# LayerNorm's turned rows from a second layout of x: a broadcast by DMA, a subtraction on GpSimd, a product on VectorE

## What is computed

```python
mod = (silu(c) @ wmod).reshape(2, 6, 1, -1)      # sa, ca, ga, sb, cb, gb
h = layernorm(x) * (1 + ca) + sa
q, k, v = silu(h @ wq), sigmoid(h @ wk), h @ wv
f = 1 - k                                        # decay; its sign against 0.5 gives the rotation
S = S * f + k * v; o = q * scale @ S             # scanned over 4096 rows, 4 heads of 128
out = layernorm(o * sigmoid(h @ wg1 @ wg2)) * norm_w @ wo
x = x + ga * out
h = layernorm(x) * (1 + cb) + sb
xr, xk = mixes of h and h shifted by one row
x = x + gb * sigmoid(xr @ W_r) * (relu(xk @ W_k)**2 @ W_v)
```

## Time and profile before

| | |
|---|---|
| median of 3 runs | 1790.52 us |
| profiled execution, time | 1790.45 us |
| profiled execution, span (first to last instruction) | 1788.9 us |
| TensorE's granted clock, mean | 0.999 of full speed |
| attention part | about 44 to 1193 us of the span |
| channel mix | from there to the end |

### The profile page before, as it was taken

How to read it: one execution, slowest core, us unless ns; L and a number is a source line. 1 busy time by engine, 2 the same in 40 slices (tenths; PEclk the granted TensorE clock), 3 DMA queues, 4 the chain that set the end, 5 groups by cost and what they waited for, 6 DMA issues and landing times.

```text
span 1788.9 us, 45434 instructions
## 1 busy us (share of the span) xinstructions
PE 1761.1 (98%) x18909; PEld 1583.4 (89%) x18909; DVE 1523.5 (85%) x3483; ACT 829.6 (46%) x1493; POOL 364.4 (20%) x303
## 2 busy tenths in 40 slices
PE   9999999999999999999999999998999999999999
PEld 7888888988999888988999889987888888989888
DVE  7898988989899899989899898998878777787875
ACT  4444444444444445444444444444454545454453
POOL 1000111101110011101110011102334343434443
PEclk9999999999999999999999999999999999999999
DMA  6122113211221112311121111210221212111110
GB/s 236 49 61 60 37 37 80 53 37 37 43 62 41 37 37 55 102 37 37 43 55 48 37 37 43 67 49 36 83 71 49 71 48 71 52 67 60 60 60 36
DMA packets 107700, 102.02 MB, mean 57 GB/s; under 512 B 65748, under 2 KB 67560, under 8 KB 107496
## 3 DMA queue, kind: packets, MB, share of 16 engines
q1 hardware_dynamic: 107480, 99.11, 19.3%
q10 hardware_dynamic: 16, 0.00, 0.0%
HBM read 48.77 MB, written 34.60 MB: 47 GB/s over the span
## 4 chain that ended last, share of the span: by engine, by line
PE 85%; DVE 9%; ACT 3%; issue 3%; DVEq 0%; ACTq 0%
PE bank L1336 60%; PE lvl L1336 9%; ACT hF L467 3%; PE bank L1450 3%; PE bank L1344 2%; PE bank L1443 2%; PE lvl L1411 2%; PE bank L1442 1%; PE bank L1434 1%; DVE xs L813 1%; DVE hT_hi L760 1%; DVE og L951 1%; PE lvl L1394 1%; PE lvl L1429 1%; DVE A L936 1%
## 5 line engine op out<-in xcount | busy, mean ns | idle before, releaser
L133 POOL TENSOR_TENSOR ln_rs<-ln_ve,mhalf 128x2 f32<-128x2 f32 x64 | 82.8, 1294 | 875.0 <-DVE ln_ve L128 875.0
L1336 PE MATMUL bank<-hT_hi,wq_hi 128*128 128x256 f32 x512 | 147.3, 288 | 11.9 <-DVE og L951 10.7
L402 POOL COPY og_halves<-og 128x1024 uint16<-128x1024 uint16 x60 | 65.3, 1089 | 407.8 <-DVE og L951 407.8
L1336 PE MATMUL bank<-hT_hi,wk_hi 128*128 128x256 f32 x512 | 148.2, 289 | 0.0
L1336 PE MATMUL bank<-xk_hi,fk_hi 128*128 128x256 f32 x512 | 145.1, 283 | 0.6 <-DVE xk_lo L1008 0.6
L1336 PE MATMUL bank<-hT_lo,wk_hi 128*128 128x256 f32 x512 | 144.9, 283 | 0.0
L1336 PE MATMUL bank<-xk_hi,fk_lo 128*128 128x256 f32 x512 | 144.9, 283 | 0.0
L1336 PE MATMUL bank<-xk_lo,fk_hi 128*128 128x256 f32 x512 | 144.9, 283 | 0.0
L1336 PE MATMUL bank<-hT_lo,wq_hi 128*128 128x256 f32 x512 | 144.7, 283 | 0.0
L1336 PE MATMUL bank<-hT_hi,wq_lo 128*128 128x256 f32 x512 | 144.7, 283 | 0.0
L1336 PE MATMUL bank<-hT_hi,wk_lo 128*128 128x256 f32 x512 | 144.7, 283 | 0.0
(11 more groups left out here) (234 smaller groups left out, 5754.0 us busy)
## 6 DMA issues: line engine op xcount, KB each, us to landing
xs<-in_L_attn_x SPq DMA_DIRECT2D x32, 512.0 KB, 4.0
x_scratch<-xs SPq DMA_DIRECT2D x32, 512.0 KB, 2.9
xs<-x_scratch SPq DMA_DIRECT2D x32, 512.0 KB, 3.6
out<-xs SPq DMA_DIRECT2D x31, 512.0 KB, 2.8
mod_raw<-in_L_wmod SPq DMA_DIRECT2D x6, 1024.0 KB, 7.2
raw_q<-in_L_attn_wq SPq DMA_DIRECT2D x2, 512.0 KB, 4.8
raw_k<-in_L_attn_wk SPq DMA_DIRECT2D x1, 1024.0 KB, 6.3
raw_v<-in_L_attn_wv SPq DMA_DIRECT2D x1, 1024.0 KB, 7.5
```

The source lines that it names most:

```text
L133: pool.tensor_tensor(out=ln["rs"][:, :], in0=ln["ve"][:, :], in1=mhalf[:, :], op=ALU.pow).then_inc(ln["rstd"], 1)
L402: pool.tensor_copy(halves[:, ch, :].rearrange("p (two e) -> p two e", two=2), og[n % 2][:, ch, :].bitcast(U16).rearrange("p (e two) -> p t ...
L1336: last = pe.matmul(dst, lhs(a, s), rhs(b, s), start=(t == 0), stop=(t == len(terms) - 1))
```

## The change

- x is also given in a second layout, turned (512 x 8192), made on the host. SP loads block n + 2 of it straight into `hF` (`xT_load`), behind the load of x.
- The statistics move up: `ln_stats` and `ln_var` for block n + 2 now stand after the second `joined_low`, before `pair_update(n, 1)`.
- Mean and 1/std of the 256 rows lie beside each other in `mvr`. SP writes them to DRAM as 512 single numbers, waits for that, and reads them back broadcast to all 128 partitions (`spread_rows`), 2 KB each.
- GpSimd subtracts the mean from `hF` in one pass of 128x1024 (`h_normal`), VectorE multiplies by 1/std in one pass of 128x1024 (`h_product`) where `apply_next` stood, ScalarE applies scale and shift in place (`h_scaled`).
- `t1` and `ln_apply` are kept only for blocks 0 and 1 and for the channel mix, whose first turning is still made in body 30.
- On TensorE the query pair 1 (bank 3) is computed before pair 0 (bank 2), and the wait for `og_sb` stands between them; ScalarE and VectorE take the pairs in that order too (`place`).

```diff
+                def xT_load(n):
+                    sp.wait_ge(h_lo, n)
+                    sp.dma_start(hF[:, :, :], xT[:, rows(n)].rearrange("(k p) t -> p k t", p=P)).then_inc(xT_in, 16)
+
+                def spread_rows(n):
+                    sp.wait_ge(ln["rstd"], n + 1)
+                    sp.wait_ge(h_lo, n)
+                    sp.dma_start(rowd[n].rearrange("(v p) -> p v", p=P), ln["mvr"][:, :, 0], allow_slow_non_contiguous=True).then_inc(row_out, 16)
+                    sp.wait_ge(row_out, 16 * (n - 1))
+                    sp.dma_start(mr[:, :, :].rearrange("p q t -> p (q t)"),
+                                 rowd[n].unsqueeze(0).to_broadcast([P, 2 * TB])).then_inc(mr_in, 16)
...
                         ln_load(sp, ln, xf if n + 2 < NB else x2d, n + 2)
+                    if n + 2 < NB:
+                        xT_load(n + 2)
...
+                    if n + 2 < NB:
+                        spread_rows(n + 2)
                     if n < LAST - 1:
                         turn_og(n, 0)
...
+                def h_normal(n):
+                    pool.wait_ge(xT_in, 16 * (n - 1))
+                    pool.wait_ge(mr_in, 16 * (n - 1))
+                    pool.tensor_tensor(out=hF[:, :, :], in0=hF[:, :, :], in1=mr[:, 0, :].unsqueeze(1).to_broadcast([P, KT, TB]),
+                                       op=ALU.subtract).then_inc(h_off, 1)
...
                     ln_rstd(pool, ln, mhalf, n + 2)
+                    if n + 2 < NB:
+                        h_normal(n + 2)
                     if n < LAST - 1:
                         og_split(n, 0)
...
+                def h_scaled(n):
+                    act.wait_ge(h_norm, n - 1)
+                    for k in range(KT):
+                        act.activation(hF[:, k, :], hF[:, k, :], ACT.Identity, scale=scl[0][:, n // BPB, k:k + 1],
+                                       bias=sft[0][:, n // BPB, k:k + 1]).then_inc(h_full, 1)
...
+                def h_product(n):
+                    dve.wait_ge(h_off, n - 1)
+                    dve.tensor_tensor(out=hF[:, :, :], in0=hF[:, :, :], in1=mr[:, 1, :].unsqueeze(1).to_broadcast([P, KT, TB]),
+                                      op=ALU.mult).then_inc(h_norm, 1)
...
+                    q_silu(n + 1, 1 - par, 1)
+                    joint(n, 1)
                     q_silu(n + 1, 1 - par, 0)
-                    joint(n, 1)
-                    q_silu(n + 1, 1 - par, 1)
                     if n > 0:
                         joined_low(n - 1, 1)
+                    ln_stats(dve, ln, n + 2)
+                    wait(dve, row_out, 16 * n)
+                    ln_var(dve, ln, n + 2)
                     pair_update(n, par, 1)
...
-                    dve.wait_ge(mm["t1"], 2 * (n + 2))
+                    if n == 0:
+                        dve.wait_ge(mm["t1"], 4)
                     f_signed(n + 1, 1 - par, 0, xn[:, 0, :])
...
-                    ln_stats(dve, ln, n + 2)
-                    ln_var(dve, ln, n + 2)
                     first_totals(n + 1)
...
-                    apply_next(n + 2)
+                    if n + 2 == NB:
+                        apply_next(n + 2)
+                    elif n + 2 < NB:
+                        h_product(n + 2)
...
                     pe.wait_ge(h_lo, n + 2)
+                    wait(pe, s_mid, n)
+                    rows_of("q", 1, 2, "q")
+                    if n == 0:
+                        mod_rows(2, bank[0])
                     wait(pe, og_sb, 2 * n)
                     rows_of("q", 0, 2, "q")
-                    wait(pe, s_mid, n)
-                    if n == 0:
-                        mod_rows(2, bank[0])
-                    rows_of("q", 1, 2, "q")
...
-                    pe.wait_ge(kt_sb, kept(n, chunks_kept(n) - 1))
-                    pe.wait_ge(gate_sb, 2 * (n + 1) + 1)
-                    t1(n + 2)
+                    if n + 2 == NB:
+                        pe.wait_ge(kt_sb, kept(n, chunks_kept(n) - 1))
+                        pe.wait_ge(gate_sb, 2 * (n + 1) + 1)
+                        t1(n + 2)
```

More of the change, by code:

```diff
@@ L51, with adaln_kernel @@
 XS = 4
-def adaln_kernel(nc, x, wq, wk, wv, wo, wg1, wg2, norm_w, W_r, W_k, W_v, mu_r, mu_k, c, wmod, out):
+def adaln_kernel(nc, x, xT, wq, wk, wv, wo, wg1, wg2, norm_w, W_r, W_k, W_v, mu_r, mu_k, c, wmod, out):
     xf = x.rearrange("b t e -> (b t) e")
@@ L58, in adaln_kernel @@
     x2d = nc.dram_tensor("x2_scratch", (B * T, E), F32, kind="Internal").ap()
+    rowd = nc.dram_tensor("row_scratch", (NB, 2 * TB), F32, kind="Internal").ap()
     base = nc.sbuf_base + (-nc.sbuf_base) % 64
@@ L124, in ln_var @@
     for ch in range(NC):
-        last = dve.bn_aggr(ln["mv"][:, ch, :], ln["st"][:, ch, :])
+        last = dve.bn_aggr(ln["mvr"][:, ch, :], ln["st"][:, ch, :])
     last.then_inc(ln["var"], 1)
     dve.wait_ge(ln["var"], n + 1)
-    dve.tensor_scalar(ln["ve"][:, :], ln["mv"][:, :, 1], EPS, None, ALU.add).then_inc(ln["ve_ready"], 1)
+    dve.tensor_scalar(ln["ve"][:, :], ln["mvr"][:, 0:NC, 1], EPS, None, ALU.add).then_inc(ln["ve_ready"], 1)
 def ln_rstd(pool, ln, mhalf, n):
     pool.wait_ge(ln["ve_ready"], n + 1)
-    pool.tensor_tensor(out=ln["rs"][:, :], in0=ln["ve"][:, :], in1=mhalf[:, :], op=ALU.pow).then_inc(ln["rstd"], 1)
+    pool.tensor_tensor(out=ln["mvr"][:, NC:2 * NC, 0], in0=ln["ve"][:, :], in1=mhalf[:, :], op=ALU.pow).then_inc(ln["rstd"], 1)
 def ln_apply(dve, ln, n):
@@ L138, in ln_apply @@
     for ch in range(NC):
-        last = dve.tensor_scalar(ln["xn"][:, ch, :], chunk(ln, n, ch), ln["mv"][:, ch, 0:1], ln["rs"][:, ch:ch + 1],
+        last = dve.tensor_scalar(ln["xn"][:, ch, :], chunk(ln, n, ch), ln["mvr"][:, ch, 0:1], ln["mvr"][:, NC + ch, 0:1],
                                  ALU.subtract, ALU.mult)
@@ L149, in closing, with place, turned @@
     return n % BPB == BPB - 1
+def place(n, pair):
+    return 2 * n + (pair if n == 0 else 1 - pair) + 1
+def turned(n):
+    return n if n < 2 else n - NB + 2
 def chunks_kept(n):
@@ L174, in blocks @@
     W, gab, scl, sft, xf, x2d, of = (env[n] for n in ("W", "gab", "scl", "sft", "xf", "x2d", "of"))
-    wod = env["wod"]
+    wod, rowd, xT = (env[n] for n in ("wod", "rowd", "xT"))
     ln, xs, xn = (env[n] for n in ("ln", "xs", "xn"))
@@ L263, in blocks @@
         og_halved, og_joined = (sem(ctx, n) for n in ("og_halved", "og_joined"))
+        xT_in, row_out, mr_in, h_off, h_norm = (sem(ctx, n) for n in ("xT_in", "row_out", "mr_in", "h_off", "h_norm"))
         og_turned = [sem(ctx, f"og_turned{ch}") for ch in range(NC)]
@@ L473, in h2_affine @@
                         if k % 2 == 0:
-                            act.wait_ge(mm["t1"], 2 * (NB + m) + k // 2 + 1)
+                            act.wait_ge(mm["t1"], 2 * turned(NB + m) + k // 2 + 1)
                         last = act.activation(h2[:, k, 1:TB + 1], banks[k // 2][:, (k % 2) * TB:(k % 2 + 1) * TB], ACT.Identity,
@@ L479, in q_gate @@
                 def q_gate(n, par, pair):
-                    act.wait_ge(mm["q"], 2 * n + pair + 1)
+                    act.wait_ge(mm["q"], place(n, pair))
                     act.activation(Q[par][:, 4 * pair:4 * pair + 4, :, :],
@@ L644, in attention_body @@
                     if n + 2 < NB:
-                        h_affine(n + 2)
+                        h_scaled(n + 2)
                     if n == 0:
@@ L765, in q_silu @@
                 def q_silu(n, par, pair):
-                    dve.wait_ge(q_sig, 2 * n + pair + 1)
+                    dve.wait_ge(q_sig, place(n, pair))
                     dst = Q[par][:, 4 * pair:4 * pair + 4, :, :]
@@ L1028, in apply_next @@
                 def apply_next(n):
-                    dve.wait_ge(mm["t1"], 2 * n)
+                    dve.wait_ge(mm["t1"], 2 * turned(n))
                     ln_apply(dve, ln, n)
@@ L1339, in turn_xn @@
                 def turn_xn(n, banks):
-                    pe.wait_ge(ln["xn_ready"], n + 1)
+                    pe.wait_ge(ln["xn_ready"], turned(n) + 1)
                     for k in range(KT):
@@ L1736 @@
     for name in _INS:
-        a = _np.asarray(inputs[name])
+        a = _np.asarray(inputs['L0_attn_x']).reshape(B * T, E).T if name == 'x_turned' else _np.asarray(inputs[name])
         a = _np.ascontiguousarray(a.T if name in _TURNED else a)
```

12 lines of the change are left out of this document (6 added, 6 removed).

## The result

The changed kernel is slower. Its median is 1835.47 us (1834.1 to 1836.28, 4 runs) against 1790.51 us of the kernel before (1789.42 to 1790.53, 4 runs): a ratio of 1.0252, 95% interval 1.0234 to 1.027. The forecast was 1766 us with a range of 1756 to 1780. What came is rival C, the detour through DRAM that is late.

The account below looks back on a forecast made before the run. TensorE (98% busy) bounds the kernel, VectorE next; with the lock VectorE's block becomes 35.82 us. 28 blocks × (36.87 − 35.82) = 29.4, less 4.8 = 24.6; 1790.45 − 24.6 gives 1766 us, range 1756 to 1780.

Parts of the forecast that it names:

- rival C: Detour of mean and 1/std through DRAM is late, `h_product` waits; slower, about 1814 us at X = 13; chance 0.11.
- X: SP's row write to DRAM, the wait for it and the broadcast read together: taken as 7.5 us, hidden.
- 11.2 us free: Time X may take, from 1/std ready to VectorE reaching `h_product`, before VectorE has to wait.
- The lock: VectorE loses time on shared SBUF ports during GpSimd's subtraction: 2.1 us per block, bounds 0 and 2.54.
- rival B: GpSimd's subtraction costs VectorE the whole 2.54 us pass or more: blocks 36.26 us, 1778 us; chance 0.16.
- work in a row: VectorE's block without its idle time: 33.49 us before the change, 33.72 us after, without the lock.
- the third of the prediction's own reasons to doubt it: Waits between TensorE and VectorE might no longer fit into each other once both run full; no size given.
- TensorE's floor: Shortest block TensorE allows: 36.87 less 0.79 (turnings) less 0.38 (wait for `og`), 35.70 us.
- rival A: GpSimd's subtraction costs VectorE nothing and TensorE's floor decides: 28 × 1.17 = 32.8 us off, 1758 us; chance 0.16.
- The query pairs: On TensorE, computing pair 1 first removes the wait of the query rows for VectorE's `og`: 0.38 us per block.
- the 1.3 us of cover: VectorE's h is ready at T + 34.4, 1.3 us before TensorE's next query rows; cost zero.
- The blocks with more work: Blocks 12 to 15 and 17 have eight more VectorE products, no longer hidden by idle time: +4.8 us.

Follow-up runs that it names:

- c_apart: Changed kernel with the 512 numbers written 64 bytes apart in DRAM and the broadcast read taken from x: 1783.55 us.
- d_nowrite: Changed kernel without the row write and the waits for it, the broadcast read taken from a row of x: 1788.42 us.
- h_late: d_nowrite with one wait more, GpSimd starting its subtraction only after VectorE has finished `q_odd`: 1761.9 us.
- f_tens: Changed kernel with mean and 1/std turned by TensorE, copied out by ScalarE and written as 4 pieces of 512 bytes: 1775.46 us.
- m_all: Changed kernel with the row write in 128 pieces of 16 bytes, rows read with that step, GpSimd subtracting behind `q_odd`: 1796.07 us.
- e_nosub: d_nowrite with GpSimd's subtraction cut from 128x1024 to 128x2: 1754.35 us.
- q_best: f_tens with the subtraction moved from GpSimd to VectorE, straight ahead of the product: 1756.77 us.
- b_pieces: Changed kernel with the row write in 128 pieces of 16 bytes in place of 512 of 4 bytes: 1774.11 us.
- i_16b: c_apart with the 512 numbers 16 bytes apart in DRAM in place of 64: 1769.43 us.
- n_dve: m_all with the subtraction on VectorE, straight ahead of the product, and none on GpSimd: 1779.8 us.

## Why the prediction was wrong, and where it was right

- **X, the way of the rows: the step that failed.** The prediction took 7.5 us, from bounds of 4 and "about 8" us, and with 11.2 us free booked its cost as zero; it was 13.8, and every block waits for what is over. The read was 5.05, close to the 4.0 of the 512 KB load. The write was mis-sized: 8.83 us, bounded by a transpose of 3.1 us. The transpose was thought near because it too has over a thousand small packets; c_apart shows that the number of packets isn't what counts. The bound came from a row that shared the wrong property. The text itself named this as the unknown without a row, and an upper end of 8 us was too firm for it.
- **Rival C's formula.** 35.82 + (X − 11.2) gives 38.4 at X = 13.77, and the median block is 38.28. The free time of 11.2 us was near: with the measured loop it is 35.82 − 22.03 − 2.4 = 11.4. Some of this is luck. 11.2 us is where the subtraction must start; the whole pass of 2.54 us behind it, against the 2.1 that were booked, would leave 10.8 us by the prediction's own terms, and a shorter power (0.8 us for 1.06) and pass (2.37) gave it back. The chance given to it, 0.11, was too small.
- **The lock.** Size right: 2.2 us (d_nowrite) and 2.06 (h_late) against 2.1, but not for the reason given. The 2.1 was twice the loss under one pass of 128x512. What the rows show is rival B's mechanism, a VectorE instruction that is held until GpSimd's pass is over; it comes out below the pass's own length (2.45 us in d_nowrite, 2.67 in h_late) because the pass had begun 0.10 or 0.46 us before the instruction. That the two sizes meet is in part luck. Nor is "work in a row" plus lock, 35.82 us, the block: at the same lock blocks were 36.6 us ahead of `q_odd` and 35.64 behind it. This is the third of the prediction's own reasons to doubt it, waits that no longer fit into each other, and it was worth 26.5 us, more than the whole forecast gain of 24.6. Even without the detour 1766 wasn't to be had at every X: d_nowrite (3.45 us from 1/std to the subtraction) took 1788, and f_tens (7.59, next to the 7.5 forecast) 1775.
- **VectorE's work in a row.** 33.72 us was 0.4 too much. m_all, where VectorE never idles, gives 36.70 − 2.59 (lock) − 0.81 (longer `h_product`) = 33.30. With the lock of 2.1 that is 35.4 us, under TensorE's floor, and so h_late stands at the floor: VectorE does not set the pace "by a hair", and behind `q_odd` the lock costs next to nothing, as rival A had it (1758; h_late took 1761.9).
- **TensorE's floor.** 35.70 forecast, 35.64 measured in h_late, e_nosub, q_best, and in the undisturbed blocks of b_pieces and i_16b. The query pairs: 0.38 forecast, 0.35 measured. The turnings: 36.52 − 35.64 = 0.88 against 0.79.
- **h is in time.** In d_nowrite, h_late, f_tens and q_best no product waits for h block after block: the 1.3 us of cover held. Where VectorE's queue is too long it doesn't: TensorE waits for the low half of h in 25 blocks of n_dve, and in 11 of the changed kernel.
- **GpSimd's pass.** 2.5 us forecast, 2.37 to 2.67 measured.
- **SP's queue.** Costs nothing, as forecast; the turnings of `og` aren't in the chain.
- **The blocks with more work.** 0.6 us for each of eight products, 4.8 in the sum, was right where VectorE sets the pace: in m_all the distances with one product more (bodies 12 to 15) are 37.58, 37.32, 37.29 and 37.30 us and that with four (body 17) 38.65, beside 36.70, together 4.6 us. In e_nosub, where VectorE has no lock, its idle time hides them, and in h_late only in part (35.93 to 36.26 and 37.35 beside 35.64), so they are part of the 7.6 us between these two.

## What to carry to other kernels

An operation of which no row exists deserves an open upper end, and the nearest row must share the property that costs. Where two engines share a resource, ask which instruction will be standing at the lock and who waits for that one, before adding up the microseconds. To turn a few numbers into a row, one matmul against the identity and a DMA with long pieces (1.29 us to completion) beats a DMA of single numbers by far.

## What the runs showed of the hardware that was not expected

- A DRAM write of 512 single numbers of 4 bytes, **side by side**, completes 8.85 us after its issue (median; 8.3 to 11.1), taken as the issue of the read that waits for it. The same numbers 16 bytes apart: 2.6 (2.5 to 3.1); 64 bytes apart: 1.9 (1.8 to 3.0); 128 pieces of 16 bytes: 1.4 (1.4 to 3.2); 4 pieces of 512: 1.2 (1.2 to 2.4). The packets of the slow one are over 1.7 us after its issue in the block shown, and the remaining 6.9 us show none of it. The Trainium skill ("DMA: Bandwidth & Descriptors", specifications) says that below 512 bytes a transfer does read-modify-write. That would fit neighbours waiting for each other, but the quick forms with pieces of 4 and 16 bytes are below 512 bytes too, and no run here shows what happens inside; the cause stays open.
- A second input with a step of 16 bytes makes a 128x1024 pass in float32 0.81 us longer on VectorE and 0.53 on GpSimd.
- While that slow write is outstanding, TensorE stops with no semaphore to wait for, even inside a product (1.76 and 2.30 us), and goes on, in most blocks, within 0.6 us of the write's completion. Only the two kernels with this write show it. The cause is open.
- A GpSimd pass over SBUF holds one VectorE instruction until it is over, less 0.11 to 0.16 us; what VectorE loses is what is left of the pass when that instruction comes, 2.1 to 2.2 us of 2.4 to 2.7 in most blocks. In the kernel before it is the same: L861 starts at 568.46, GpSimd's copy ends at 569.45, and 0.85 us are lost.
- TensorE was granted half its clock (1.2 GHz) in short stretches after it had stood still for most of 3 us (busy 0.87 of the 3 us up to 725). It cost little, since another engine set the pace.
